# A selective-scan and mixture-of-experts kernel: convolution as four shifted products on TensorE, the D term by ScalarE and transposes

## The reference, cut to what matters

```python
xz = x @ W_in                                   # 128 -> 512
xs, z = jnp.split(xz, 2, axis=-1)               # 256 channels each
xc = silu(causal_conv(xs, conv_w, taps=4) + conv_b)
dbl = xc @ W_x                                  # 64 + 16 + 16
dt = softplus(dbl[..., :64] @ W_dt + b_dt)
Bm, Cm = dbl[..., 64:80], dbl[..., 80:]
h = exp(dt * A) * h + dt * xc * Bm              # 16 states, along the tokens
y = sum over the states of h * Cm + xc * D_param
y = (y * silu(z)) @ W_out
```

## Time and profile before

| | |
|---|---|
| median of 3 runs | 1222.59 us (1222.11 to 1223.76) |
| the profiled execution | 1228.98 us |
| its span, first to last instruction | 1227.1 us |
| PE busy | 919.4 us, 75% |
| DVE busy | 967.1 us, 79% |
| ACT busy | 610.6 us, 50% |
| POOL busy | 594.1 us, 48% |
| mean granted clock of PE | 0.874 |

### The profile page before, as it was taken

One profiled execution on the slowest core, in us unless ns is written; L12 is line 12 of the kernel. 1 busy time (PEld: TensorE's weight loads), 2 busy tenths in 40 slices (PEclk: granted clock), 3 DMA queues, 4 the chain that ended last, 5 costly groups with the idle time before them and its releaser, 6 DMA issues.

```text
span 1227.1 us, 16938 instructions
## 1 busy us (share of the span) xinstructions
PE 919.4 (75%) x4540; PEld 650.9 (53%) x4540; DVE 967.1 (79%) x1808; ACT 610.6 (50%) x1585; POOL 594.1 (48%) x420
## 2 busy tenths in 40 slices
PE   2277587877677778876887889778676788889678
PEld 0054366545455555555655566556454565566456
DVE  4298689987998988877988797969658886888455
ACT  1343554563556545653665465645445554655233
POOL 0036523767436633785336333784774646335500
PEclk9676798896899988898998899988878897989888
DMA  8924334455434434553544534355644356445201
GB/s 263 284 73 105 101 86 98 136 141 140 120 104 112 110 85 108 141 139 117 121 95 115 123 97 112 108 159 133 152 115 113 79 117 167 103 110 133 66 5 31
DMA packets 168650, 144.71 MB, mean 118 GB/s; under 512 B 15680, under 2 KB 135536, under 8 KB 168560
## 3 DMA queue, kind: packets, MB, share of 16 engines
q10 hardware_dynamic: 39168, 67.12, 24.0%
q1 hardware_dynamic: 121712, 60.78, 17.4%
q0 software_dynamic: 7680, 15.74, 4.0%
...
...
## 4 chain that ended last, share of the span: by engine, by line
PE 30%; DVE 28%; issue 15%; POOL 11%; ACT 7%; SPq 4%; DMA 3%; another core or an unknown queue 1%; ACTq 1%; DVEq 0%; POOLq 0%
DVE pA L1305 10%; PE pM L919 5%; POOL dBx L738 5%; PE pH L829 3%; PE pM L909 3%; DVE hj L1341 3%; POOL rows_in L696 3%; PE p L884 3%; POOL gy L712 3%; PE pG L881 2%; PE pU L882 2%; SPq L594 2%; DVE hj L1353 2%; PE pG L884 1%; PE pH L897 1%
## 5 line engine op out<-in xcount | busy, mean ns | idle before, releaser
L738 POOL TENSOR_TENSOR dBx<-dtx,bcb 128x1024 f32<-128x1024 f32 (+1 forms) x144 | 305.7, 2123 | 453.7 <-DVE pA L1305 405.0
L829 PE MATMUL pH<-const,hc 128*128 128x128 f32 x1024 | 165.9, 310 | 55.2 <-DVE hc L1313 49.3
L1305 DVE TENSOR_TENSOR_SCAN pA<-pA,carry,dBx 128x512 f32<-128x512 f32 (+1 forms) x160 | 162.9, 1064 | 43.8 <-ACT pA L939 22.5
L939 ACT ACTIVATE pA<-dt,am 128x512 f32<-128x512 f32 (+1 forms) x288 | 173.9, 639 | 27.4 <-DVE hc L1313 19.0
L1305 DVE TENSOR_TENSOR_SCAN pA<-pA,dBx 128x512 f32<-128x512 f32 x128 | 149.8, 1216 | 38.7 <-POOL dBx L738 25.3
L829 PEld LDWEIGHTS pH<-const,hc 128*128 128x128 f32 x1024 | 131.2, 159 | 76.5 <-DVE hc L1313 57.4
L909 PE MATMUL pM<-const,hj 128*128 128x128 f32 (+3 forms) x636 | 131.5, 304 | 46.5 <-ACT hT L1114 13.3
L1313 DVE TENSOR_TENSOR hc<-pA,bcb 128x1024 f32<-128x1024 f32 (+1 forms) x144 | 159.3, 1106 | 5.0
L696 POOL DMA_INDIRECT rows_in<-xn,slots x120 | 127.4, 1062 | 30.4 <-issue 27.5
L909 PEld LDWEIGHTS pM<-const,hj 128*128 128x128 f32 (+3 forms) x636 | 74.2, 142 | 120.5 <-issue 82.2
L1111 ACT ACTIVATE yj<-pM 128x128 f32<-128x128 f32 x236 | 65.3, 277 | 137.7 <-PE pM L919 117.6
...
## 6 DMA issues: line engine op xcount, KB each, us to landing
bcb<-bc_rows ACTq DMA_DIRECT2D x112, 512.0 KB
...
```

The source lines that it names most:

```text
L738: pool.tensor_tensor(dBx[:, N % 2, :, 0:t1 - t0], dtx[q % 2][:, :, t0:t1], row, ALU.mult).then_inc(dBx_ready, 1)
L829: last = mm(pH[:, half, c * DI + k * P:c * DI + (k + 1) * P], hc[:, N % 2, k, t * P:(t + 1) * P], ident, is_transpose=True, start=(n == 0 ...
L939: A(pA[:, k, 0:t1 - t0], dt[q % 2][:, k, t0:t1], ACT.Exp, scale=am[:, k, n:n + 1]).then_inc(decay_ready, 1)
L1305: dve.tensor_tensor_scan(pA[:, k, 0:w], pA[:, k, 0:w], dBx[:, N % 2, k, 0:w], carry[:, k, N % NS:N % NS + 1] if N in carry_after else 0.0, ...
```

## The change

The input weights of the x part are multiplied with each of the four taps (`wtap`, one DVE operation at the start, from taps broadcast over the partitions by their load). A convolved half of 256 tokens is then four products with shifted views of the normalised input, accumulated in the bank. There are four such pieces for each chunk, in the steps n = 2 to 5, and ACT makes `ca` and its Tanh from the bank directly. The tensor `xs`, the items `conv` and `thc`, and the clears of all banks but one are gone. D times xc is made by ACT (two operations) into the free `dtx` buffer, and is transposed by PE into `pH` in the segment's step n = 1, so that `y` is one DVE operation that reads `pH`. ACT makes e + 1 after the Ln, into the `dtx` that the chunk will fill. PE runs eight products on zeros while the loads come in. `xc` has one buffer instead of two.

```diff
     def mixer_front(q, s):
-        at(s, "xs", q, 0)
-        at(s + 1, "xs", q, 1)
-        at(s + 2, "conv", q, 0)
-        at(s + 3, "conv", q, 1)
-        at(s + 3, "thc", q)
+        for k in range(DK):
+            for h in range(2):
+                at(s + 2 * k + h, "xs", q, k, h)
...
+    for s in range(len(SEGS)):
+        at(NS * s + 1, "dxc", s)
...
-            (cw[:], T["L0_attn_conv_w"].rearrange("(k p) j -> p k j", p=P)),
+            (cwb, T["conv_taps"].rearrange("(o j) d -> o j d", o=1).broadcast_to([P, 4, DI])),
...
+                    pe.wait_ge(zero_tile, 1)
+                    for c in range(8):
+                        last = mm(pU[:], gy[:, 0, 0, :], gy[:, 0, 4 * (c % 2):4 * (c % 2) + 4, :].rearrange("p c d -> p (c d)"),
+                                  start=True, stop=True)
...
+                elif kind == "xs":
+                    q, k, h = a
+                    if q == k == h == 0:
+                        pe.wait_ge(prepared, 2)
+                    take(kind, q, k, h)
+                    t0, n = q % 2 * HALF + h * HALF // 2, HALF // 2
+                    for j in (3, 2, 1, 0):
+                        skip = 3 - j if t0 == 0 else 0
+                        last = mm(pM[:, skip:n], wtap[:, j, k * P:(k + 1) * P], xnT[0, q // 2][:, t0 + skip - (3 - j):t0 + n - (3 - j)],
+                                  start=(j == 3), stop=(j == 0))
+                    last.then_inc(bank_full, 1)
...
+                elif kind == "dxc":
+                    s, = a
+                    pe.wait_ge(dxc_ready, s + 1)
+                    for c in range(seg_tiles(s)):
+                        for k in range(DK):
+                            last = mm(pH[:, c // 2, c % 2 * DI + k * P:c % 2 * DI + (k + 1) * P], dxc_of(s)[:, k, c * P:(c + 1) * P], ident,
+                                      is_transpose=True, start=False, stop=False, skip_group_check=True)
                     last.then_inc(hflip_full, 1)
...
-                    A(xs[:, k, 3:3 + HALF], pM[:], ACT.Copy)
-
-                    A(ca[:, k, :], pM[:], ACT.Identity, scale=cw[:, k, 3:4], bias=cb[:, k:k + 1]).then_inc(bank_read, 1)
...
-                    A(v[:], ca[:], ACT.Tanh).then_inc(thc_ready, 1)
+                    t = slice(h * HALF // 2, (h + 1) * HALF // 2)
+                    A(ca[:, k, t], pM[:, 0:HALF // 2], ACT.Identity, bias=cb[:, k:k + 1])
+                    A(v[:, k, t], pM[:, 0:HALF // 2], ACT.Tanh, bias=cb[:, k:k + 1]).then_inc(bank_read, 1)
+                elif kind == "dxc":
+                    s, = a
+                    q, t0, t1 = SEGS[s]
+                    act.wait_ge(xc_ready, q + 1)
+                    act.wait_ge(dBx_ready, NS * s)
+                    for k in range(DK):
+                        last = A(dxc_of(s)[:, k, :], xc[:, k, t0:t1], ACT.Copy, scale=dpar[:, k:k + 1])
+                    last.then_inc(dxc_ready, 1)
...
-                    A(dt[q % 2][:], ca[:], ACT.Ln, bias=1.0).then_inc(ln_ready, 1)
+                    A(dt[q % 2][:], ca[:], ACT.Ln, bias=1.0)
+                    if q:
+                        act.wait_ge(hflip_full, flips_before(NS * (q - 1) + 2))
+                    A(dtx[q % 2][:], ca[:], ACT.Identity, bias=1.0).then_inc(ln_ready, 1)
...
-            for t in (pA, pH, pG, pU, p1, pM):
-                dve.memset(t[:], 0.0)
-            dve.memset(xs[:], 0.0)
+            dve.memset(pM[:], 0.0)
...
-                    for j in (2, 1, 0):
-                        last = dve.scalar_tensor_tensor(out=ca[:, k, :], in0=xs[:, k, j:j + HALF], scalar=cw[:, k, j:j + 1],
-                                                        in1=ca[:, k, :], op0=ALU.mult, op1=ALU.add)
...
-                    link(dve.tensor_scalar(g, ca[:], 1.0, None, ALU.add))
-                    link(dve.scalar_tensor_tensor(out=g, in0=g, scalar=1.0, in1=ca[:], op0=ALU.subtract, op1=ALU.subtract))
-                    link(dve.tensor_tensor(g, dt[q % 2][:], g, ALU.subtract))
+                    link(dve.scalar_tensor_tensor(out=ca[:], in0=dtx[q % 2][:], scalar=1.0, in1=ca[:], op0=ALU.subtract, op1=ALU.subtract))
+                    link(dve.tensor_tensor(ca[:], dt[q % 2][:], ca[:], ALU.subtract))
...
-                    for k in range(DK):
-                        last = dve.scalar_tensor_tensor(out=y[:, k, 0:w], in0=xc[q % 2][:, k, t0:t1], scalar=dpar[:, k:k + 1],
-                                                        in1=acc_half(s, k), op0=ALU.mult, op1=ALU.add)
-                    link(last)
-                    dve.scalar_tensor_tensor(out=y[:, :, 0:w], in0=y[:, :, 0:w], scalar=0.5, in1=zs[:, :, t0:t1], op0=ALU.mult, op1=ALU.mult
+                    total = pH[:].rearrange("p h t -> p (h t)")[:, 0:DK * w].rearrange("p (k t) -> p k t", k=DK)
+                    dve.scalar_tensor_tensor(out=y[:, :, 0:w], in0=total, scalar=0.5, in1=zs[:, :, t0:t1], op0=ALU.mult, op1=ALU.mult
                                              ).then_inc(y_ready, 1)
```

More of the change, by code:

```diff
@@ L218, in make_plan @@
         at(max(last[1, b] + 2, STEPS + 5), "outd", b)
-    plan = [("xload", 0), ("norm", 0, 0), ("xn", 0, 0), ("xT", 0, 0, 0), ("xs", 0, 0), ("xT", 0, 0, 1), ("xs", 0, 1),
-            ("conv", 0, 0), ("conv", 0, 1), ("thc", 0), ("xc", 0), ("dbl", 0), ("dtr", 0, 0), ("dtr", 0, 1),
+    plan = [("xload", 0), ("norm", 0, 0), ("xn", 0, 0), ("xT", 0, 0, 0), *(("xs", 0, k, h) for k in range(DK) for h in range(2)),
+            ("xT", 0, 0, 1), ("xc", 0), ("dbl", 0), ("dtr", 0, 0), ("dtr", 0, 1),
             ("soft", 0), ("ln", 0), ("dt", 0)]
@@ L431, in program @@
         zs = sb("zs", [P, DK, HALF])
-        xc = [sb(f"xc{i}", [P, DK, HALF]) for i in range(2)]
+        xc = sb("xc", [P, DK, HALF])
         dt = [sb(f"dt{i}", [P, DK, HALF]) for i in range(2)]
@@ L809, in _ @@
                     for k in range(DK):
-                        last = mm(pM[0:R + 2 * NS, :], w_x[:, k, :], xc[q % 2][:, k, :], start=(k == 0), stop=(k == DK - 1))
+                        last = mm(pM[0:R + 2 * NS, :], w_x[:, k, :], xc[:, k, :], start=(k == 0), stop=(k == DK - 1))
                     last.then_inc(bank_full, 1)
@@ L830, in _ @@
                                           is_transpose=True, start=(n == 0 and c == k == 0), stop=(n == NS - 1), skip_group_check=True)
+                    last.then_inc(hflip_full, 1)
+                elif kind == "dxc":
[5 more added lines that the diff above has]
+                                      is_transpose=True, start=False, stop=False, skip_group_check=True)
                     last.then_inc(hflip_full, 1)
@@ L1152, in _ @@
             dve.wait_ge(mix_loaded, 16 * len(mix_loads))
-            dve.tensor_scalar(cw[:], cw[:], 0.5, None, ALU.mult)
+            dve.scalar_tensor_tensor(out=wtap[:], in0=cwb, scalar=0.5,
+                                     in1=w_in[:, 0:DI].rearrange("p (o d) -> p o d", o=1).broadcast_to([P, 4, DI]), op0=ALU.mult, op1=ALU.mult)
             dve.tensor_scalar(cb[:], cb[:], 0.5, None, ALU.mult)
@@ L1445 @@
     arrays["conv_b"], arrays["b_dt"], arrays["D_param"] = (half(inputs["L0_attn_" + n]) for n in ("conv_b", "b_dt", "D_param"))
+    arrays["conv_taps"] = np.ascontiguousarray(np.asarray(inputs["L0_attn_conv_w"]).T)
     arrays["gate0T"] = np.ascontiguousarray(np.asarray(inputs["L0_ffn_gate_w"]).T)
```

59 lines of the change are left out of this document (22 added, 37 removed).

## The result

The changed kernel takes 1235.12 us (median of 4 runs, 1232.7 to 1242.12), the kernel before 1222.41 (4 runs, 1222.11 to 1223.76): a ratio of 1.011, 95% interval 1.007 to 1.015. It is slower by 1.1%. I had predicted 1211.6 us, in a range of 1188 to 1234. The sign was wrong, and the time lies outside the range.

A forecast was written before the change was run, and what follows sets the result against it. No single bound: the chain passes between PE (30%) and DVE (28%). Terms -9 + 2 - 10 - 2 + 7 + 1 = -11 us, about 1218 for a profiled execution, adjusted to a 1211.6 us median; range 1188 to 1234.

The forecast's parts named there:

- The convolution: 48 DVE operations removed, products added on PE: 1.8 us gained in each of five chunks, -9 us (0 to -22).
- the first two steps: Steps n = 2 and 3 of a chunk: 0.85 us more PE work each, 14 times; +2 us (0 to +12).
- I take 1.8 us in each of five chunks: Convolution gain in step 37's kind: scan 1.8 us earlier, not 2.3; two of seven chunks excluded; -9 us.
- all of the gain is gone: Step 37: the new 1.7 us of products go ahead of PE's 1.85 us router product; taken to meet two chunks.
- y: L1321, L1324: two 741 ns DVE operations go in seven chunks, half-width ones in two segments; -10 us (-5 to -14).
- The port: Last y operation reads one operand from PSUM; if freed from GpSimd contention, two chunks give 1.2 us each.
- dt: L1284: one 1379 ns DVE operation goes in seven chunks, ACT gets a 1.06 us Identity; -2 us (-10 to +3).
- The D term: Step n = 1 of each segment: PE transposes wait for ACT's product; 0.8 us by nine segments, +7 us (0 to +31).
- The start: Shorter front, removed clears and warm-up hidden by some 10 us; larger taps load costs +1 us (-1 to +3).
- PE takes DVE's place: Rival, chance 0.23: convolution gives 0, first two steps +6, D term +12; total +7, 1230 us.
- its "against": Argument against the 1230 us rival: PE no longer waits for DVE through the convolution, so its clock should fall less often.
- signs of being right: DVE near 912 us, PE near 968; n = 0 about 1 us shorter, n = 5 1 to 2, n = 4 unchanged.

The follow-up runs named there:

- conv_only: The kernel before with only the convolution moved to TensorE, ca and Tanh by ScalarE: 1237.35 us, ratio 1.014 to the kernel before.
- dterm_only: The kernel before with only the D term moved (product by ScalarE, transposes into pH, y one VectorE operation): 1224.63 us, ratio 1.001.
- eone_only: The kernel before with only e+1 made by ScalarE instead of VectorE: 1218.14 us, ratio 0.997 to the kernel before.
- d_and_e: The changed kernel with its convolution back on VectorE; D term, e+1 and shorter start stay: 1219.39 us, ratio 0.999 to the kernel before.
- pieces_last: The changed kernel with each convolution piece issued as the last item of its step, still n = 2 to 5: 1236.85 us, ratio 1.004 to before.

## Why the prediction was wrong, point by point

- **The convolution, -9 (0 to -22), and the first two steps, +2.** Together -7; measured alone +14.8 (conv_only). This is the step that failed, and with it the sum: the new products were taken to fit behind the transposes at a cost of nothing or less, and in four of seven chunks they lengthened PE's queue instead. Its links:
  - "I take 1.8 us in each of five chunks": it held in three (-3.0, -1.8, -3.0 us). The other fronts stand beside the pieces in four chunks, and I had looked for the router's product alone, in two. The transposes count as well as the router.
  - "all of the gain is gone" and "0 if PE has no gap anywhere": I cut the term off at zero, with no reason that excludes a loss. Where PE has no room, a piece of 2.0 us and its bank turn of 0.9 lengthen the step. With these prices, measured only afterwards, and the right chunks, the same working gives an estimate of 4 x (2 x 2.9 - 1.8) - 3 x 1.8 = +11 us; n = 4 to 6 of after have +13.3.
  - "PE's 5.91 us plus 1.7 are 7.6 of today's 7.70: nothing to gain": the sum of busy time in a window says nothing about where its gap lies. Of before, two rows of step 36 show it: PE's gap stands ahead of the second gate product, and the transposes, behind which the piece comes in the queue, run at the end of the step (the next scan starts at 338.91).

```profile
335.91 0.85 PE L881 MATMUL pG<-w13a,xgT 128*128 x2 [1.60 <-DVE hj L1353]
...
338.30 1.04 PE L829 MATMUL pH<-const,hc 128*128 128x128 f32 x8
```

  - "four reads ... I count that as nothing, since ACT is half idle": the reads of 256 columns take 0.47 us each, not less than the 0.46 us of 352 columns, and PE waits for both with a full queue behind it. An engine's mean load doesn't tell whether another waits for it.
  - The first two steps were right: conv_only has -0.8 and +1.2 at n = 2 and 3.
  - The products were priced at 1.7 us a piece and took 1.89 to 2.00 at full clock. The 0.21 us of a pass came from the difference between two widths, which leaves out what a pass costs at any width; the same two rows give 0.51 - 0.21 = 0.30 for a whole pass of 256 columns, and 0.24 was measured.
- **y, -10.** n = 0 is 7.4 us shorter in after, 6.9 in dterm_only. Six whole y stand in these steps, two of them beside a GpSimd operation; the forecast for them was 6 x 1.0 + 2 x 1.2 = 8.4, so the term was about right. The port: in step 64 before, y took 2.44 us beside a GpSimd operation. The same place in after, where the two overlap again:

```profile
550.43 1.22 DVE L1337 SCALAR_TENSOR_TENSOR y<-pH,zs 128x1024 f32<-128x1024 f32 x1
550.85 2.36 POOL L746 TENSOR_TENSOR dBx<-dtx,bcb 128x1024 f32<-128x1024 f32 x1
```

  None of the nine takes more than 1225 ns. The form that reads one operand from PSUM isn't held up, and the GpSimd operation keeps its 2.36 us. Here y started first; in step 64 before, an operation of L1321, which also reads one operand from PSUM, began at 551.26 inside the GpSimd operation and still took 740 ns. That is what the Trainium skill ("SBUF — State Buffer", "SBUF: two separate sides") says of a VectorE operation without two SBUF inputs, and the trace agrees.
- **dt, -2 (-10 to +3).** eone_only is faster by 4.4 us of the medians (0.9 to 6.7 by the interval). n = 12, where the group stands, has only 0.9 of it. There is no second table load behind the Ln, just as it had been forecast with the Trainium skill ("ScalarE: Activation LUTs", "Table sets: the hidden batching unit"); the groups of eone_only show eight loads at the Ln's line for eight chunks, none at the Identity's, and the Identity at 1040 ns. The next Tanh still needs its own, 15 loads in all as before:

```profile
L1086 ACT ACT_TABLE_LOAD x8 | 10.3, 1283 | 0.1
...
L1087 ACT ACTIVATE dtx<-ca 128x1024 f32<-128x1024 f32 x8 | 8.3, 1040 | 0.0
```

- **The D term, +7 (0 to +31).** The wait of about 2.4 us was there, and transposes of 1.09 us. n = 2 got 10.4 us longer in dterm_only, 1.5 us for each of seven, where I had taken 0.8 (5.6 in all); but in after and d_and_e, with the same D term, it is +4.8 and +5.7. By the medians, y and D together are +2.1 us in dterm_only (interval -2.2 to +4.5) against a forecast of -3. Right mechanism; the size was between right and some 5 us too cheap.
- **The start, +1.** Right, it is hidden: the first scan starts at 61.47 (61 to 63 forecast), because the store of dbl is issued at 48.11 only, 8.4 us after dbl is ready, as before. The front itself isn't shorter, though I had thought so: ACT starts dbl at 39.09 against 38.47, and the first two of its four pieces run at the lower clock (0.50), 3.73 and 3.78 us each:

```profile
20.42 3.73 PE L821 MATMUL pM<-xnT,wtap 128*128 128x256 f32 x8 [0.84 <-ACT xnT L995]
...
39.09 0.59 ACT L1069 ACTIVATE dbl<-pM 96x512 f32<-96x512 f32 x1 [2.11 <-PE pM L834]
...
48.11 1.57 SPq L606 DMA_DIRECT2D bc_rows<-dbl  x1
...
61.47 1.23 DVE L1321 TENSOR_TENSOR_SCAN pA<-pA,dBx 128x512 f32<-128x512 f32 x1 [7.33 <-POOL dBx L746]
```

- **The rivals.** *PE takes DVE's place*, 1230 us at 0.23, was nearest and named the right engine. But it too set the convolution at 0 and got its loss from the first two steps and the D term, partly by a lower clock. The clock fell less often, as its "against" said: the mean is 0.893, and 218 to 223 us is at 1.00 where it was 0.58. Its point of decision ("PE's gap behind the transposes of hc is shorter than 1.7 us") was the right one to look at, and I had the rows to look at it chunk by chunk.
- **Signs named beforehand.** Steps n = 2 to 5 longer together than before was to mean that PE had taken over: they are 4.2 us longer in after. Steps n = 1 and 2 longer by more than 1.5 us were to mean that the D term's wait isn't hidden: they are 4.7 us longer in seven chunks, 0.7 each, so that sign stayed off. Of the signs of being right, n = 0 and the waits for the D product came; n = 5, forecast 1 to 2 us shorter in a chunk, is 0.6 longer, and n = 4, forecast unchanged, is 0.7 shorter. n = 6 was on no list of mine, since no piece has that number; the queue carried the loss there.

## What to carry to other kernels

Work that is moved to an engine with an in-order queue must be laid beside that queue's own items, in every chunk, and not beside its mean load or its idle sum: find where in the order the gap lies, and what else shares the buffer. Where two engines covered each other (DVE's convolution beside PE's router), moving the one onto the other adds both, so the bound of such a term lies on the side of a loss. And when a moved part loses time in one known step, move it to other steps before giving it up: here the moves of the pieces and of the D transposes together were worth 41 and 48 us on one chip (1242.01 against 1201.47 and 1194.18).

## What the runs showed beyond that

- A hand-over of a PSUM bank from PE to ACT and back costs PE about 0.93 to 1.02 us of waiting for two reads of 256 columns (0.47 us each, overlapping), and 1.52 us when ACT is in another operation.
- Chips differ by as much as the change: the same kernel before has medians of 1221.11 (19 runs), 1221.33 (7), 1222.57 (25) and 1233.32 us (16) on four chips. pieces_last has a ratio of 1.004 on one chip and 1.012 on another.
- A single profiled execution can lie 6.6 us off its median, spread over steps that nothing had touched. Differences that every other kernel shows in the same steps are the mark of it.
